# A LoRA-plus-cross-attention kernel: router logits from x in two groups, last query copies over two steps, last tile's Newton step on ScalarE

## The reference

```python
# x: 4 x 512 x 1024, ctx: 4 x 64 x 1024
a_sum  = x @ sum(A)                              # 64 columns; A is a part of ctx
w      = softmax(x @ router_W.T + router_b)      # 8 columns
x      = nan_to_num(x + 0.5 * sum_n w[n] * (a_sum @ B[n].T))
Q, K, V = x @ Wq.T + bq, ctx @ Wk.T + bk, ctx @ Wv.T + bv     # 32 heads of 32
attn   = softmax(where(mask, Q K^T / sqrt(32), -inf))
z      = x + (attn V) @ Wo.T + bo
out    = (z - mean(z)) / sqrt(var(z) + 1e-5) * ln_g + ln_b
```

## Time and profile before

| | |
|---|---|
| median of 3 runs | 638.55 us (638.39 to 639.22) |
| the profiled execution, its own time | 638.67 us |
| its span, first to last instruction | 636.8 us |
| PE busy | 627.9 us, 99% |
| DVE, ACT, POOL busy | 499.5, 338.3, 267.7 us |
| granted PE clock, mean | 0.998 of full speed |

### The profile page before, as it was taken

One profiled execution on the slowest core, in us unless ns is written; L12 is line 12 of the kernel. 1 busy time (PEld: TensorE's weight loads), 2 busy tenths in 40 slices (PEclk: granted clock), 3 DMA queues, 4 the chain that ended last, 5 costly groups with the idle time before them and its releaser, 6 DMA issues.

```text
span 636.8 us, 10729 instructions
## 1 busy us (share of the span) xinstructions
PE 627.9 (99%) x3455; PEld 544.9 (86%) x3455; DVE 499.5 (78%) x907; ACT 338.3 (53%) x1000; POOL 267.7 (42%) x358
## 2 busy tenths in 40 slices
PE   9999999999999999999999999999999999999995
PEld 8988889888988889888888888888888888888884
DVE  6689995578457773677668899999999999999834
ACT  5453463123242232422258777777778877777621
POOL 0120001000030002000325556788899888888956
PEclk9999999999999999999999999999999999999999
DMA  8936695436874467721857993524355354523132
GB/s 313 411 127 173 178 303 180 163 83 202 241 265 152 115 220 243 285 96 47 259 144 278 372 383 107 149 99 157 100 134 175 97 176 110 154 96 117 60 106 100
DMA packets 103399, 114.14 MB, mean 179 GB/s; under 512 B 57008, under 2 KB 76080, under 8 KB 103344
## 3 DMA queue, kind: packets, MB, share of 16 engines
q1 hardware_dynamic: 103008, 113.07, 53.9%
q10 hardware_dynamic: 336, 0.39, 0.2%
HBM read 67.29 MB, written 46.14 MB: 178 GB/s over the span
## 4 chain that ended last, share of the span: by engine, by line
PE 94%; SPq 2%; DMA 1%; DVE 1%; issue 1%; POOL 0%; DVEq 0%; ACT 0%; POOLq 0%
PE ps L604 26%; PE ps L606 26%; PE ps L605 26%; PE ps L672 4%; PE ps L755 4%; PE ps L768 2%; PE ps L769 2%; DMA x_sb<-xT 1%; PE ps L682 1%; SPq L390 1%; SPq L393 0%; PE ps L643 0%; PE ps L644 0%; PE ps L646 0%; DVE cx_sum L995 0%
## 5 line engine op out<-in xcount | busy, mean ns | idle before, releaser
L1280 POOL TENSOR_TENSOR u_sb<-a_sb,w_sb 128x512 f32<-128x512 f32 x16 | 19.6, 1247 | 234.9 <-DVE w_sb L893 230.0
L604 PE MATMUL ps<-wo_hi,cx_hi 128*128 128x512 f32 (+1 forms) x264 | 105.9, 401 | 0.0
L1206 ACT ACTIVATE s_sb<-s_sb,s_min 128x64 f32<-128x64 f32 x256 | 85.8, 338 | 32.3 <-DVE s_min L973 32.3
L606 PE MATMUL ps<-wo_hi,cx_lo 128*128 128x512 f32 (+1 forms) x264 | 101.7, 385 | 0.0
L605 PE MATMUL ps<-wo_lo,cx_hi 128*128 128x512 f32 (+1 forms) x264 | 101.6, 385 | 0.0
L604 PE MATMUL ps<-act_hi,w_hi 128*128 128x512 f32 x256 | 100.7, 393 | 0.0
L605 PE MATMUL ps<-act_lo,w_hi 128*128 128x512 f32 x256 | 99.8, 390 | 0.0
L606 PE MATMUL ps<-act_hi,w_lo 128*128 128x512 f32 x256 | 99.8, 390 | 0.0
L1171 ACT ACTIVATE act_hi<-h_t 128x512 fp32r<-128x512 f32 x32 | 20.3, 633 | 111.6 <-DVE h_t L936 111.6
L995 DVE SCALAR_TENSOR_TENSOR cx_sum<-ps,bias_c,cx_raw 64x256 f32<-64x256 f32 x128 | 61.8, 483 | 8.7 <-ACT cx_raw L1220 4.8
L1292 POOL TENSOR_TENSOR s_sb<-s_sb,s_inv 128x512 f32<-128x512 f32 x64 | 67.0, 1048 | 0.0
(11 more groups left out here) (123 smaller groups left out, 1538.5 us busy)
## 6 DMA issues: line engine op xcount, KB each, us to landing
q_cols<-q_sb SPq DMA_DIRECT2D x32, 512.0 KB, 3.3
qb<-q_cols SPq DMA_DIRECT2D x64, 256.0 KB, 3.9
x_sb<-xT SPq DMA_DIRECT2D x32, 256.0 KB, 3.1
h_rows<-hn_sb SPq DMA_DIRECT2D x64, 128.0 KB, 2.9
output_weights<-wo_sb SPq DMA_DIRECT2D x32, 256.0 KB, 3.1
z_sb<-h_rows SPq DMA_DIRECT2D x16, 512.0 KB, 4.7
out<-z_sb SPq DMA_DIRECT2D x15, 512.0 KB, 2.9
stage<-WvT SPq DMA_DIRECT2D x8, 512.0 KB, 4.7
```

The lines of the kernel that those rows point to most:

```text
L604: pe.matmul(dst, lh, rh, start=(first and j == 0), stop=False)
L606: mm = pe.matmul(dst, ll, rh, start=False, stop=(last and j == n - 1))
L1206: act.activation(s_sb[c % 4][:, h, :], s_sb[c % 4][:, h, :], ACT.Exp, bias=s_min[c % 2][:, h:h + 1], scale=-1.0, accum_out=s_sum[c % 2][:, ...
```

## The change

Three edits that don't touch the same code.

A. For element 0 alone, x's first four chunks signal a semaphore of their own (`x_first`), and the 64 matmuls of the logits run in two groups: chunks 0 to 3 for all four token tiles, then chunks 4 to 7. The whole bank is one accumulation: one start, one stop.

B. `pair_out` of pair 1 is cut in two: its first block's copies stay at the end of what precedes step 13, the second block's move to before step 14. For pair 0 both stay where they were. Output projection o = 0 waits for all copies but the last, o = 1 (step 16) for all.

C. Newton's step is written in fewer operations: POOL now starts from -0.5 (var + eps), which needs no guess; then for tiles 0 to 14 it does two more operations instead of three. For the last tile ACT does the rest: Square of the guess, an Identity with two per-partition operands, a Copy with a per-partition scale. A constant 1.5 per partition is set by POOL at the start.

```diff
-        left[6 + n] = [("pair", pair, 2 * k), ("pair", pair, 2 * k + 1)] + ([("pair_out", pair)] if k == 3 else [])
+        left[6 + n] = [("pair", pair, 2 * k), ("pair", pair, 2 * k + 1)] + ([("pair_out", pair, 0)] if k == 3 else [])
+    left[9] += [("pair_out", 0, 1)]
+    left[14] = [("pair_out", 1, 1)]
...
-                sp.dma_start(x_sb[:, c, :], x_v[i, c]).then_inc(x_in, 16)
+                sp.dma_start(x_sb[:, c, :], x_v[i, c]).then_inc(x_first if i == 0 and c < KC // 2 else x_in, 16)
...
-            def pair_out(pair):
-                if pair == 0:
+            def pair_out(pair, j):
+                if pair == 0 and j == 1:
                     store_pair(0)
...
-                pe.wait_ge(x_in, 16 * KC * (i + 1))
-                wait(pe, ulo_done, TT * i)
+                if i == 0:
+                    for part in range(2):
+                        pe.wait_ge(x_first if part == 0 else x_in, 16 * KC // 2)
+                        for t in range(TT):
+                            for k in range(4 * part, 4 * part + 4):
+                                mm = pe.matmul(ps_al[:, t, :], x_sb[:, k, t * P:(t + 1) * P], a_rhs[:, k, :],
+                                               start=(t == 0 and k == 0), stop=(t == TT - 1 and k == KC - 1))
+                    mm.then_inc(al_mm, 1)
+                    return
+                pe.wait_ge(x_in, 16 * KC * i + 16 * KC // 2)
+                pe.wait_ge(ulo_done, TT * i)
...
-                    if o == 0:
-                        pe.wait_ge(q_copied, ALL)
+                    if o < 2:
+                        pe.wait_ge(q_copied, ALL - 1 + o)
...
-            def pair_out(n):
-                for j in range(2):
-                    q_low(ALL - 4 + 2 * n + j, 2 + j, ALL - 4 + 2 * n + j)
+            def pair_out(n, j):
+                q_low(ALL - 4 + 2 * n + j, 2 + j, ALL - 4 + 2 * n + j)
...
+            def last_deviation(n):
+                act.wait_ge(guess_done, n + 1)
+                act.activation(log_var[:], guess[:], ACT.Square).then_inc(last_newton, 1)
+                act.wait_ge(last_newton, 1)
+                act.wait_ge(nudge_done, 2 * n + 1)
+                act.activation(nudge[:], nudge[:], ACT.Identity, bias=half_three[:, 0:1], scale=log_var[:, 0:1]).then_inc(last_newton, 1)
+                act.wait_ge(last_newton, 2)
+                wait(act, norm_done, n)
+                act.wait_ge(offset_done, n)
+                act.activation(rstd[:], guess[:], ACT.Copy, scale=nudge[:, 0:1]).then_inc(rstd_done, 1)
...
             def newton(n):
+                pool.wait_ge(ag_done, n + 1)
+                wait(pool, rstd_done, n)
+                pool.tensor_scalar(nudge[:], mv[:, 1:2], EPS, -0.5, ALU.add, ALU.mult).then_inc(nudge_done, 1)
+                if n == TILES - 1:
+                    return
                 pool.wait_ge(guess_done, n + 1)
-                pool.tensor_scalar(nudge[:], mv[:, 1:2], EPS, guess[:, 0:1], ALU.add, ALU.mult).then_inc(nudge_done, 1)
...
+                pool.tensor_scalar(nudge[:], nudge[:], guess[:, 0:1], guess[:, 0:1], ALU.mult, ALU.mult).then_inc(nudge_done, 1)
+                pool.wait_ge(nudge_done, 2 * n + 2)
                 wait(pool, norm_done, n)
-                pool.tensor_tensor(rstd[:], nudge[:], guess[:], ALU.mult).then_inc(rstd_done, 1)
+                pool.tensor_scalar(rstd[:], nudge[:], 1.5, guess[:, 0:1], ALU.add, ALU.mult).then_inc(rstd_done, 1)
```

More of the change, by code:

```diff
@@ L227, in xattn_kernel @@
         eps_c = sb("eps_c", [P, 1])
+        half_three = sb("half_three", [P, 1])
         mask_f = sb("mask_f", [P, NB, V])
@@ L318, in xattn_kernel @@
         ident_set, ident_ready, warm_set = sem("ident_set"), sem("ident_ready"), sem("warm_set")
-        small_in, mask_in, x_in = sem("small_in"), sem("mask_in"), sem("x_in")
+        small_in, mask_in, x_first, x_in = sem("small_in"), sem("mask_in"), sem("x_first"), sem("x_in")
         rw_in, rb_in = sem("rw_in"), sem("rb_in")
@@ L359, in xattn_kernel @@
         gain_done, out_ready = sem("gain_done"), sem("out_ready")
-        last_gain, last_out = sem("last_gain"), sem("last_out")
+        last_gain, last_out, last_newton = sem("last_gain"), sem("last_out"), sem("last_newton")
         res_in = [sem(f"res_in{k}") for k in range(4)]
@@ L1183, in exit_high, with pair_out @@
                     q_high(KC * i + 4 * g + j, j, KC * i + 4 * g + place)
-            def pair_out(n):
-                for j in range(2):
-                    q_high(ALL - 4 + 2 * n + j, 2 + j, ALL - 4 + 2 * n + j)
+            def pair_out(n, j):
+                q_high(ALL - 4 + 2 * n + j, 2 + j, ALL - 4 + 2 * n + j)
             def output_weight(n):
@@ L1236, in inverse_deviation @@
                 act.activation(guess[:], log_var[:], ACT.Exp, scale=-0.5).then_inc(guess_done, 1)
+                if n == TILES - 1:
+                    last_deviation(n)
             def normalise(n):
@@ L1271, in _ @@
             pool.memset(eps_c[:], EPS).then_inc(ident_set, 1)
-            pool.wait_ge(ident_set, 2)
+            pool.memset(half_three[:], 1.5).then_inc(ident_set, 1)
+            pool.wait_ge(ident_set, 3)
             pool.affine_select(out=ident[:], in_=ident[:], compare_op=ALU.not_equal, fill=1.0, base=0,
@@ L1302, in newton @@
             def newton(n):
-                pool.wait_ge(guess_done, n + 1)
-                pool.tensor_scalar(nudge[:], mv[:, 1:2], EPS, guess[:, 0:1], ALU.add, ALU.mult).then_inc(nudge_done, 1)
[L1305 to L1310, removed]
-                pool.tensor_tensor(rstd[:], nudge[:], guess[:], ALU.mult).then_inc(rstd_done, 1)
+                pool.wait_ge(ag_done, n + 1)
+                wait(pool, rstd_done, n)
+                pool.tensor_scalar(nudge[:], mv[:, 1:2], EPS, -0.5, ALU.add, ALU.mult).then_inc(nudge_done, 1)
                 if n == TILES - 1:
                     return
+                pool.wait_ge(guess_done, n + 1)
+                pool.wait_ge(nudge_done, 2 * n + 1)
+                pool.tensor_scalar(nudge[:], nudge[:], guess[:, 0:1], guess[:, 0:1], ALU.mult, ALU.mult).then_inc(nudge_done, 1)
+                pool.wait_ge(nudge_done, 2 * n + 2)
+                wait(pool, norm_done, n)
+                pool.tensor_scalar(rstd[:], nudge[:], 1.5, guess[:, 0:1], ALU.add, ALU.mult).then_inc(rstd_done, 1)
                 pool.wait_ge(rstd_done, n + 1)
```

## The result

| | before | after |
|---|---|---|
| median, 22 runs each | 638.80 us | 637.67 us |
| profiled execution, own time | 638.67 us | 637.45 us |
| its span | 636.8 us | 635.7 us |

The ratio is 0.9984 with a 95% interval of 0.9979 to 0.9990: 1.0 us less, between 0.6 and 1.3 (the two medians lie 1.13 apart). The forecast was 0.96 us less, 637.6.

The account below looks back on a forecast made before the run. The prediction took PE to bound the kernel, with gains only at few PE waits and in the tail. Terms 0.10 + 0.21 + 0.65 = 0.96 us off 638.55 gave 637.6 us, range 637.0 to 638.4.

Parts of the forecast that it names:

- The bound: Between 40 and 317 us and 372 and 629 us PE is always busy; only less PE work could help there.
- A, at its first step: At the first logits, PE's 0.40 us wait for x moves to POOL's second product before the fifth transpose; gain nothing.
- A, 0.10 one stage later: ACT's second transpose copy starts 0.11 us earlier, shrinking PE's 0.11 stall before the first update; gain taken 0.10 us.
- The stall before the context product: In step 14 PE waits 0.21 us for DVE's p_low; moving one copy later removes it, gain 0.21 us.
- The price: Moved copies delay DVE's next p_low in step 14; 0.5 us of slack before PE wants it hides them.
- C: Last tile's chain to DVE's final pair gets shorter, gain 0.65 us; tiles 0 to 14 cost and gain nothing.
- the dead heat: Last tile: POOL's variance product and DVE's gain multiply start together; gain 0.57 us if POOL is held, otherwise 0.73.
- 1 (A in full): Router follows the logits if B0 and B1 land earlier, both early stalls go, 0.51 us; total 637.2 us, chance 0.15.
- 2 (a table load for Square): At the kernel's end ACT loads another table between exponential and Square; slower, 638.9 us, chance 0.08.
- 3 (only the tail pays): DVE makes step 14's next context product late and POOL meets DVE at 33 us; only 0.57 gained, 638.0 us, chance 0.15.

Follow-up runs that it names:

- a_alone: The kernel before with only edit A, the logits in two groups: 638.89 us, ratio 1.0000 to the kernel before.
- filler: The whole change with two unused matmuls added on PE right before the first logits: 637.87 us, ratio 0.9982 to the kernel before.
- after_again: The whole change run once more, unaltered: 637.75 us, ratio 0.9984 to the kernel before.
- b_alone: The kernel before with only edit B, the later query copy: 638.50 us, ratio 0.9999 to the kernel before.
- b_and_c: The whole change without edit A: 637.91 us, ratio 0.9982 to the kernel before.
- product_late: The whole change, but POOL's product of the variance waits for ACT's guess in all tiles: 637.83 us, ratio 0.9980 to the kernel before.
- stores_late: The whole change with pair 0's two stores moved to step 15, behind the output weights' loads: 637.74 us, ratio 0.9981 to the kernel before.
- pair0_split: The whole change with pair 0's second block's copies also moved, to before step 10: 643.84 us, ratio 1.0077 to the kernel before.

## Why the prediction was right, point by point

**The bound.** Right. 251.27 us of the second phase are the same in every kernel, and no profile shows a new PE gap between the first update and the first scores.

**A, at its first step, right.** The wait moves from x to POOL's product, and A is worth nothing there; a_alone (a gap of 0.73) and filler (1.12) show it as well. The prediction said 0.5 us between the fourth and the fifth weight load, leaving at 33.2. In the profile of the change it was 0.21, as the clock rose late; in after_again, with an early rise, 0.97, leaving at 33.30.

**A, 0.10 one stage later, wrong.** The step that failed is that ACT's second copy waited for the first. It started at 33.94 before and at 33.99 in after_again, with the first at 33.41 and 32.74: it waits for the eighth transpose, which POOL holds. The stall before the update stays, 0.11 before and 0.09 in after_again (40.09 to 40.41 instead of 40.32), and U follows the router by 12.16 in every profile with the router in its old place but the one where PE was last. The term of 0.10 measured 0.

**B, mechanism right, the stall sized too small, the room too large.** The stall before the context product was put at 0.21. It is 0.32: when PE has stood for a weight load, the next matmul is late too (0.22 instead of 0.11, in the earlier trace rows's stretch), and that goes as well. Laid matmul by matmul beside the trace before, PE gains 0.21 and 0.11 at this place in every profile with B.

The price was looked for in DVE, whose next p_low was given 0.5 us of room. It had much less, in the trace of the change:

```profile
372.14 0.64 DVE L1000 TENSOR_TENSOR p_lo<-ps,p_hi 128x512 fp32r<-128x512 f32 x1
372.94 0.28 PE L783 MATMUL ps<-p_hi,vbd 128*128 128x256 f32 x1
```

The piece is done at 372.78, 0.16 before PE starts on it, and 0.16 or 0.17 in b_alone, b_and_c, product_late and stores_late; in the kernel before it was 0.69. PE comes 0.32 earlier, and DVE 0.22 later (372.91 in b_alone against 372.69), which fits its standing 0.38 for ACT's high part twice now and not once. That DVE cost nothing was narrower than the forecast had it, and in part luck.

What did cost, in some executions, is the transfer of the last output weight. It landed between 370.8 and 373.0 where the stores were in their old place (pair0_split aside), and in after_again PE wanted it at 372.3. It took 0.71 us in after_again (0.60 and the 0.11 behind it), 0.15 in filler and nothing in the other four profiles with B and the old stores: 0.14 in the mean of six. So B is worth 0.32 where the transfer is in time and 0.18 in that mean, which two profiles carry. The means of S say about the same (59.70 in seven with B, 59.89 in five without), but by chance: they also hold waits for query blocks, which are not B's.

**C, right.** 0.65 forecast, 0.68 measured in every profile with C but product_late. Two errors of size cancelled: the step from ACT to DVE takes 0.11 and not 0.04 (631.63 to 631.74), and POOL wins the dead heat (630.19 against 630.20), which the prediction had counted half. The mechanism was right; that the size came within 0.03 is luck. POOL's product was off the path throughout. By the Trainium skill's rule of exclusion ("SBUF — State Buffer", section "SBUF: two separate sides") POOL, starting first, pays nothing and DVE waits for it. The trace agrees with the first half: 0.19 us, as in the other fifteen tiles. The second half it doesn't show: DVE's pair started 0.01 after POOL's product and took 1.41 us, against 1.42 before.

**Sum.** 0 + 0.18 to 0.32 + 0.68 = 0.86 to 1.00 against the forecast 0.96 and the measured 1.0. That the forecast was met so closely is luck in part: the 0.10 too much for A and the 0.11 too little for B's stall cancel.

**Rivals.** 1 (A in full) fell by U and filler; its condition, a router that follows the logits, was met in none of the eleven profiles, though B1 landed up to 0.2 us earlier than in the kernel before. 2 (a table load for Square) fell: Square took 0.20 us right behind Exp, with no load between. 3 (only the tail pays) was half right: what is late next in step 15 exists, but it is a transfer, and only in some executions; DVE missed being it by 0.16.

## What to carry to other kernels

A wait that a profile shows on the bounding engine is worth nothing if what lies behind it is released by another chain: before taking a wait away, look for the next instruction whose release doesn't depend on it, and how much room it has. Deferring work past a point is as safe as the first user of its buffer is far: two steps were enough for pair 1, none was too few for pair 0. Where engines are planned to tenths of a microsecond, ask of each gain which transfer it will meet next, and when that lands in several executions, not in one.

## What the runs showed of the hardware

- TensorE's clock rose to full between 4.1 and 7.2 us after the start in the thirteen executions profiled, and PE was ready for the first logits anywhere from 19.1 to 20.2. A wait seen in one profile there may not exist in the next.
- In a stall of 3.9 us in mid-kernel (347.6 to 351.5) the granted clock fell to half at 350.6 and came back at 357.4, 5.9 us after PE had gone on.
- Where PE stood for a weight load in the second phase, the matmul behind the late one was late by 0.11 more: 0.21 and 0.11, 0.18 and 0.11, 0.60 and 0.11.
- Beside DVE's low parts, which read two SBUF operands, POOL's product took 2.02 us instead of 1.04, and the low parts took 1.89 and 2.06 instead of 1.23.
- The transfers move the whole kernel: the router's start followed the landing of B1 by 2.25 or 2.26 us and spread from 27.99 to 28.69 where its place was the old one.
